# Hartley-transform layer and Sobel layer on one core: a straight and folded first pass, a reordered second pass

## The chip, the cores and the metric

The kernel runs on one core of one Trainium2 chip. The metric is the device time of the core in microseconds (us), the median over runs. TensorE, VectorE, ScalarE, GpSimd and SyncE appear in the profile as PE, DVE, ACT, POOL and SP; PEld is TensorE loading weights.

## The reference

The input x is 32 x 64 planes of 128 x 128 float32 pixels. Two layers are added to it, one behind the other:

```
def reference(x, L0_conv_weights1):
    x = x + _L0_conv_ref(_gn(x), L0_conv_weights1)
    x = x + _L1_conv_ref(_gn(x))
    return x
```

`_gn` is a group norm over pairs of planes. The first layer takes a normalised 2-D Hartley transform of each plane, keeps 20 x 20 modes, mixes them over the channels with the weights and transforms back. The second is a depthwise Sobel filter: the square root of the sum of the squares of the two directional derivatives, and 1e-8.

## The kernel before

Three stages follow each other: `pass1` reads every plane and makes its modes and sums, `mix` mixes the modes, `pass2` reads every plane again, adds the first layer, filters and stores. Each stage is a block with one program per engine; semaphores order them. Rows of a plane lie on the 128 partitions.

**pass1** goes over 16 tiles of 128 planes, each in 8 chunks of 16 planes, each chunk in 2 halves (g). Per chunk TensorE does `first_axis` for both halves (L334, into t_ps), a share of the tile before's `second_axis` (L312, into r_ps) and `mirror` for both halves (L343, L345, into z_ps). ScalarE writes the high parts m_hi (L383), the squares (L415) and the copy of t_ps into tmodes (L419). GpSimd writes the low parts m_lo (L279). VectorE sums the squares (L458), multiplies the plane with z_ps into `prod` (L461) and, once per chunk, sums `prod` (L465); once per tile it has the edges (L440 to L449). SyncE loads a chunk ahead into one of 4 slots of xbuf when the chunk's sum is done (L267). All engines run `over_tiles`: tile 0 written out, a hardware loop of 7 rounds of two tiles, tile 15 written out.

**pass2** goes over 256 steps of 8 planes, 32 steps to a pair of tiles. All engines run `over_steps`: step 0, then a loop of 3 rounds of 64 steps, then 63 steps written out. In step r

- TensorE does `second_axis(r+3)` (L962, into v_ps), `first_axis(r+2)` (L974, into y_ps), `across` of step r for halves 0 and 1 (L982), in some steps four `transposes` of coefficients (L950, into the same bank as v_ps), and `down` of step r for both halves (L982). `across(r)` waits for the remainder p_lo of step r, `down(r, h)` for `finish(r-1, h)`.
- ScalarE does `high(r+1)` (L1035, pairs into p_hi), `copy_v(r+3)` (L1041), the squares of across (L1048) and down (L1054) for both halves, and the `roots` (L1061), two operations for each half.
- VectorE does `finish(r-1)` for both halves (L1135, two operations each), `centre(r+2)` (L1104, adds y_ps to the planes), in steps 1 to 11 of a pair `copy_coef` (L1097), in steps 16 to 23 one of eight `coefficients` operations (L1119 to L1125), and `add` for both halves (L1110).
- GpSimd does `low(r+1)` (L924, the remainder: pairs minus p_hi into p_lo) and then `neighbours(r+2)` (L919, the sum of neighbouring columns, into the one buffer `pairs`), which waits for `centre(r+2)` and for its own remainder.
- SyncE stores step r when both halves are finished and loads step r+8 into the same slot.

The orders that matter are these:

```
            def step(i, r):                      # GpSimd, L927
                if not beyond(i, r + 1):
                    low(i, r + 1)
                if not beyond(i, r + 2):
                    pool.wait_ge(lo_ready, at(i, r) + 2)
                    neighbours(i, r + 2)
```

Of the kernel before, what the change touches and what calls it, by code (L numbers as in the profile page):

```python
# [54 lines left out]
COEF_STEP = 16  # L55
# [134 lines left out]
def pass1(nc, sb, ps, sem, mat, x_p, mats, first, xbuf, modes, rows, late, small, mats_d, first_d, second_d):  # L190

    ctx = ExitStack()
    with ctx:
# [6 lines left out]
        prod = sb(ctx, "prod", [128, 2, CHUNK, 64])  # L200

# [25 lines left out]
        mirrored = sem("p1_mirrored")  # L227
        edge_muled = sem("p1_edge_muled")
# [28 lines left out]
        def _(sp):  # L257
# [6 lines left out]
            with sp.Fori(0, NCHUNK // SLOTS - 1) as j:  # L264
                for s in range(SLOTS):

                    sp.wait_ge(chunk_done, j * SLOTS + s + 1)  # L267
                    load_chunk(sp, xbuf[:, s], x_p, j * SLOTS + s + SLOTS, x_in[s])

        @block.gpsimd  # L270
        def _(pool):
            for part in (x_hi, x_lo):
                nc.gpsimd.memset(part[:, :, :, 0:RIGHT:RIGHT - 1].bitcast(FP32), 0.0).then_inc(padded, 1)

            def tile(i, par):
                for k in range(CHUNKS):
                    for g in range(2):
# [3 lines left out]
                                                x_hi[:, g, :, 1:65].bitcast(FP32), ALU.subtract).then_inc(lo_ready, 1)  # L281

            over_tiles(pool, tile)

        @block.tensor
        def _(pe):
# [74 lines left out]
            over_tiles(pe, tile)  # L361
# [66 lines left out]
        def _(dve):  # L428
# [21 lines left out]

            def tile(i, par):
                for k in range(CHUNKS):
                    slot = k % SLOTS
                    xs = xbuf[:, slot]
                    for g in range(2):
# [4 lines left out]
                        dve.wait_ge(pe_mirror, i * HALVES + 2 * k + g + 3)  # L460
                        nc.vector.tensor_tensor(prod[:, k % 2, HALF * g:HALF * (g + 1), 0:64],  # L461
                                                xs[:, HALF * g:HALF * (g + 1), 0:64][:, :, ::-1],
                                                z_ps[g][:], ALU.mult).then_inc(mirrored, 1)
# [6 lines left out]
            over_tiles(dve, tile)  # L470
            edges(TILES - 1, 1)
# [320 lines left out]
def pass2(nc, sb, ps, sem, mat, x_p, out_p, mats, xpad, modes, rows, corner, mscale, x_in):  # L792

    ctx = ExitStack()
    with ctx:
# [9 lines left out]
        pairs = sb(ctx, "pairs", [128, HALF, W + 2])  # L805
# [22 lines left out]
        pe_t0 = sem("p2_pe_t0")  # L828
# [45 lines left out]
        def group(i, r):  # L874

            g = r % PSTEPS - 1
# [34 lines left out]
        def _(pool):  # L911
# [4 lines left out]
            def neighbours(i, r):  # L916
                pool.wait_ge(centred, at(i, r) + 1)
                plane = xpad[:, r % XSTEPS]
                nc.gpsimd.tensor_tensor(pairs[:, :, 0:W + 1], plane[:, :, 0:W + 1], plane[:, :, 1:W + 2],  # L919
                                        ALU.add).then_inc(paired, 1)  # L920

            def low(i, r):
                pool.wait_ge(hi_ready, at(i, r) + 1)
                nc.gpsimd.tensor_tensor(p_lo[:, r % 2, :, 0:W + 1], pairs[:, :, 0:W + 1],  # L924
                                        p_hi[:, r % 2, :, 0:W + 1].bitcast(FP32), ALU.subtract).then_inc(lo_ready, 1)
# [9 lines left out]
            neighbours(0, 0)  # L935
            low(0, 0)
            pool.wait_ge(lo_ready, 1)
            neighbours(0, 1)
# [3 lines left out]
        def _(pe):  # L942
            def transposes(i, r, g):

                t = pair_of(i, r) + 1
                if g == 0:
                    pe.wait_ge(coef_ready, t + 1)
# [49 lines left out]
            pe.wait_ge(coef_ready, 1)  # L997
            for g in range(TGRP):
# [5 lines left out]
                mm.then_inc(pe_t0, 1)  # L1004
# [8 lines left out]
            def step(i, r):  # L1013
                s = r % PSTEPS
# [12 lines left out]
            over_steps(pe, step)  # L1027

        @block.scalar
        def _(act):  # L1030
            def high(i, r):
# [3 lines left out]
                nc.scalar.activation(p_hi[:, r % 2, :, 0:W + 1], pairs[:, :, 0:W + 1], ACT.Copy).then_inc(hi_ready, 1)  # L1035
# [28 lines left out]

            for g in range(1, TGRP, 2):
                act.wait_ge(pe_t0, g + 1)
# [8 lines left out]
            def step(i, r):  # L1075
                if not beyond(i, r + 1):
                    high(i, r + 1)
                if not beyond(i, r + 3):
                    copy_v(i, r + 3)
# [3 lines left out]
                square_down(i, r, 1)  # L1083
                roots(i, r, 0)
# [5 lines left out]
        def _(dve):  # L1090
            V = nc.vector

            def copy_coef(i, r, g):
                t = pair_of(i, r) + 1
                n = min(4, NB - 4 * g)
                dve.wait_ge(pe_t, (t - 1) * TGRP + g + 1)
# [15 lines left out]
            def coefficients(t, part, q):  # L1112

                n = MODES
                m = modes[:, bass.ds(2 * t + q, 1), :].rearrange("p t (a b) -> p (t a) b", b=n)
# [78 lines left out]
```

## Time and profile before

| | |
|---|---|
| median of 3 runs | 2515.53 us (2514.56 to 2516.2) |
| profiled execution, its own time | 2515.18 us |
| its span | 2513.4 us |
| TensorE busy | 2273.2 us, 90% |
| VectorE busy | 1955.9 us, 78% |
| ScalarE busy | 1953.2 us, 78% |
| GpSimd busy | 1456.1 us, 58% |
| mean granted clock of TensorE | 0.965 |

The span is that from the first to the last instruction. Shares are of the span. A row of the timeline gives the start and the duration in us, the engine, the line, the operation, what it writes and reads, how many like it follow each other (x4: four), and in brackets how long the engine had been idle before it and what ended that. "issue" is a wait for nothing that the profile shows, as for the engine's own instructions. Operations of one engine overlap a little, so that starts, not durations, give the pace.

### The profile page before, as it was taken

The numbers are of one execution on the slowest core, as the hardware profiler recorded it, in microseconds if no ns is written. First come the engines' busy times: TensorE is split into PE (matmuls) and PEld (weight loads), VectorE is DVE, ScalarE is ACT, GpSimd is POOL, SyncE is SP. The second block draws the span as 40 slices with busy tenths as digits, with TensorE's granted clock in tenths as the row PEclk, the third lists the DMA queues.
The fourth block names the chain that finished last, engine by engine and source line by source line (L and its number), as shares of the span: only waits on it lengthen the run. The fifth ranks groups of instructions, "written<-read, shape, count | busy, mean of one in ns | idle before, by whom it ended". The sixth has DMA issues, their size and how long they took to land.

```text
span 2513.4 us, 61005 instructions
## 1 busy us (share of the span) xinstructions
PE 2273.2 (90%) x21212; PEld 1618.4 (64%) x21212; DVE 1955.9 (78%) x2781; ACT 1953.2 (78%) x3633; POOL 1456.1 (58%) x788
## 2 busy tenths in 40 slices
PE   5988988988992687999999999999999999999998
PEld 4777777777782674666665666666666666666665
DVE  5988988988996157887886887887787888877776
ACT  6877877877873325888888888888788888889998
POOL 3433434433433024677676677677677677777776
PEclk9999999999995888999999999999999999999999
DMA  7767666666656321566556566566566556566664
GB/s 204 201 168 202 180 171 190 186 170 185 187 152 131 80 69 51 165 179 180 167 175 176 160 183 180 162 179 185 156 179 178 169 176 182 170 182 180 193 189 138
DMA packets 808903, 421.67 MB, mean 168 GB/s; under 512 B 20912, under 2 KB 807344, under 8 KB 807472
## 3 DMA queue, kind: packets, MB, share of 16 engines
q1 hardware_dynamic: 808624, 417.86, 58.4%
q8 instruction: 186, 3.05, 0.5%
q14 instruction: 93, 0.76, 0.1%
HBM read 283.56 MB, written 134.22 MB: 166 GB/s over the span
## 4 chain that ended last, share of the span: by engine, by line
POOL 21%; ACT 16%; PE 13%; issue 8%; DVE 3%; ACTq 1%; POOLq 0%; DVEq 0%
POOL p_lo L924 12%; POOL pairs L919 9%; PE g_ps L982 9%; ACT p_hi L1035 6%; ACT g_ps L1054 3%; ACT v_sb L1041 3%; DVE g_ps L1110 2%; ACT g_ps L1061 2%; PE v_ps L950 2%; ACT gx L1048 2%; PE y_ps L974 1%; PE v_ps L962 1%; ACTq L1061 0%; ACTq L1045 0%; ACTq L1034 0%
## 5 line engine op out<-in xcount | busy, mean ns | idle before, releaser
L982 PE MATMUL g_ps<-p_hi,stencil 128*128 128x512 f32 x2048 | 867.4, 424 | 16.6 <-DVE xbuf L1135 13.2
L924 POOL TENSOR_TENSOR p_lo<-pairs,p_hi 128x1032 fp32r<-128x1032 f32 x256 | 620.6, 2424 | 387.4 <-ACT p_hi L1035 387.4
L982 PE MATMUL g_ps<-p_lo,stencil 128*128 128x512 f32 x2048 | 818.9, 400 | 0.0
L982 PEld LDWEIGHTS g_ps<-p_hi,stencil 128*128 128x128 f32 x2048 | 387.4, 189 | 339.8 <-issue 158.1
L279 POOL TENSOR_TENSOR m_lo<-xbuf,m_hi 128x512 fp32r<-128x512 f32 x256 | 305.5, 1194 | 438.7 <-ACT m_hi L383 438.7
L919 POOL TENSOR_TENSOR pairs<-xbuf 128x1032 f32<-128x1032 f32 x256 | 488.1, 1906 | 52.9 <-POOL p_lo L924 30.9
L1110 DVE TENSOR_TENSOR g_ps<-gx,g_ps 128x512 f32<-128x512 f32 x512 | 339.4, 692 | 218.5 <-ACT g_ps L1054 217.3
L1135 DVE SCALAR_TENSOR_TENSOR xbuf<-xbuf,rows,g_ps 128x256 f32<-128x256 f32 x1024 | 431.7, 477 | 93.0 <-ACT g_ps L1061 78.6
L1061 ACT ACTIVATE g_ps<-g_ps,rows 128x256 f32<-128x256 f32 x1024 | 401.6, 446 | 112.2 <-DVE g_ps L1110 101.6
L982 PEld LDWEIGHTS g_ps<-p_lo,stencil 128*128 128x128 f32 x2048 | 388.8, 190 | 77.0
L334 PE MATMUL t_ps<-first_sb,xbuf 128*64 128x64 f32 x8192 | 297.9, 229 | 87.8 <-issue 40.4
L334 PEld LDWEIGHTS t_ps<-first_sb,xbuf 128*64 128x64 f32 x8192 | 266.8, 142 | 148.8 <-issue 111.5
L1054 ACT ACTIVATE g_ps<-g_ps 128x512 f32<-128x512 f32 x512 | 288.2, 596 | 85.2 <-PE g_ps L982 85.2
L458 DVE TENSOR_REDUCE rows<-square 128x1024 f32 (+1 forms) x256 | 310.2, 1212 | 43.5 <-ACT square L415 43.5
L1104 DVE TENSOR_TENSOR xbuf<-xbuf,y_ps 128x1024 f32<-128x1024 f32 x256 | 310.8, 1214 | 5.9 <-PE y_ps L974 5.9
L1035 ACT ACTIVATE p_hi<-pairs 128x1032 fp32r<-128x1032 f32 x256 | 274.0, 1070 | 40.5 <-POOL pairs L919 36.1
L1048 ACT ACTIVATE gx<-g_ps 128x512 f32<-128x512 f32 x512 | 278.5, 605 | 2.4 <-PE g_ps L982 2.4
L415 ACT ACTIVATE square<-xbuf 128x1024 f32<-128x1024 f32 x256 | 268.0, 1047 | 5.7 <-DVE rows L458 5.7
L974 PE MATMUL y_ps<-v_sb,mats_sb 41*128 41x512 f32 x1024 | 265.8, 596 | 2.8 <-DVE xbuf L1104 2.8
L383 ACT ACTIVATE m_hi<-xbuf 128x512 fp32r<-128x512 f32 x256 | 161.6, 632 | 105.7 <-PE z_ps L345 105.7
L419 ACT ACTIVATE tmodes<-t_ps 128x328 f32<-128x328 f32 x256 | 188.9, 738 | 30.0 <-PE t_ps L334 30.0
L461 DVE TENSOR_TENSOR prod<-xbuf,z_ps 128x512 f32<-128x512 f32 x256 | 173.4, 677 | 43.7 <-PE z_ps L345 43.7
(114 smaller groups left out, 2341.8 us busy)
## 6 DMA issues: line engine op xcount, KB each, us to landing
xbuf<-x SPq DMA_DIRECT2D x256, 512.0 KB, 5.2
xbuf<-x SPq DMA_DIRECT2D x512, 256.0 KB, 3.1
out<-xbuf SPq DMA_DIRECT2D x512, 256.0 KB, 2.7
xbuf<-weights SPq DMA_DIRECT2D x8, 800.0 KB, 11.5
wmix<-weights SPq DMA_DIRECT2D x8, 800.0 KB, 13.9
second_sb<-second SPq DMA_DIRECT2D x1, 1230.0 KB, 8.4
mats_sb<-mats SPq DMA_DIRECT2D x1, 704.0 KB, 6.4
first_sb<-first SPq DMA_DIRECT2D x1, 32.0 KB, 5.5
```

The costliest lines, as they stand in the source:

```text
L334: mm = nc.tensor.matmul(t_ps[g][side, p, :], xbuf[:, k % SLOTS, HALF * g + p, side], first[:], start=True, stop=True)
L458: nc.vector.tensor_reduce(rows[:, 1, bass.ds(i, 1), p0:p0 + HALF], square[:, g], axis=AX.X, op=ALU.add).then_inc(summed, 1)
L919: nc.gpsimd.tensor_tensor(pairs[:, :, 0:W + 1], plane[:, :, 0:W + 1], plane[:, :, 1:W + 2], ALU.add).then_inc(paired, 1)
L924: nc.gpsimd.tensor_tensor(p_lo[:, r % 2, :, 0:W + 1], pairs[:, :, 0:W + 1], p_hi[:, r % 2, :, 0:W + 1].bitcast(FP32), ALU.subtract).then_i ...
L982: mm = nc.tensor.matmul(g_ps[h][:, axis], stencil[:, m, :], p[:, r % 2, 4 * h:4 * h + 4, o:o + W], start=n == 0, stop=n == len(todo) - 1)
L1035: nc.scalar.activation(p_hi[:, r % 2, :, 0:W + 1], pairs[:, :, 0:W + 1], ACT.Copy).then_inc(hi_ready, 1)
L1048: nc.scalar.activation(gx2[:, h], g_ps[h][:, 0].rearrange("p n w -> p (n w)"), ACT.Square)\
L1054: nc.scalar.activation(f, f, ACT.Square).then_inc(squared_down, 1)
L1061: a = nc.scalar.activation(f, f, ACT.Sqrt, bias=EPS_SOBEL, scale=inv_var[:, bass.ds(group_planes(i, r, h, k), 1)])
L1104: V.tensor_tensor(xs, xs, y_ps[:], ALU.add).then_inc(centred, 1)
L1110: V.tensor_tensor(f, gx2[:, h], f, ALU.add).then_inc(added, 1)
L1135: v = V.scalar_tensor_tensor(xs, xs, mean[:, bass.ds(group_planes(i, r, h, k), 1)], g_ps[h][:, 1, 2 * k:2 * k + 2], ALU.add, ALU.add)
```

## The change

In the first pass TensorE's program is written out for all tiles; GpSimd folds `prod` to half its width (`fold`), a chunk behind, and VectorE sums the folded tile, also a chunk behind; SyncE's loads wait for the products and no longer for the sums. In the second pass TensorE's program is written out; `coefficients` goes to ScalarE, into steps 0 to 7 of a pair and for the next pair, between the squares and the roots (the first pair's are shared by VectorE and ScalarE before the loop); the transposes and their copies go to steps 10 to 20; ScalarE does `copy_v` ahead of `high`; `pairs` has two buffers, and GpSimd does the sum of step r+2 ahead of the remainder of step r+1; VectorE does `centre` between the two halves of `finish`. The core of the diff:

```diff
-COEF_STEP = 16
+COEF_STEP = 0
+T_STEP = 10
...
+        folded = sb(ctx, "folded", [128, 2, CHUNK, 32])
...
-                    sp.wait_ge(chunk_done, j * SLOTS + s + 1)
+                    sp.wait_ge(mirrored, (j * SLOTS + s + 1) * 2 + 2)
...
+            def fold(i, k):
+                pool.wait_ge(mirrored, i * HALVES + 2 * k + 4)
+                if not (is_first(i) and k < 2):
+                    pool.wait_ge(chunk_done, i * CHUNKS + k - 1)
+                p = prod[:, k % 2]
+                nc.gpsimd.tensor_tensor(folded[:, k % 2], p[:, :, 0:32], p[:, :, 32:64], ALU.add).then_inc(fold_done, 1)
...
+                    if k:
+                        fold(i, k - 1)
+                    elif not is_first(i):
+                        fold(i - 1, CHUNKS - 1)
...
-            over_tiles(pe, tile)
+            for i in range(TILES):
+                tile(i, i % 2)
...
+            def sums(i, k):
+                dve.wait_ge(fold_done, i * CHUNKS + k + 1)
+                nc.vector.tensor_reduce(rows[:, 0, bass.ds(i, 1), CHUNK * k:CHUNK * (k + 1)],
+                                        folded[:, k % 2], axis=AX.X, op=ALU.add).then_inc(chunk_done, 1)
...
-                    dve.wait_ge(mirrored, i * HALVES + 2 * k + 4)
-                    nc.vector.tensor_reduce(rows[:, 0, bass.ds(i, 1), CHUNK * k:CHUNK * (k + 1)],
-                                            prod[:, k % 2], axis=AX.X, op=ALU.add).then_inc(chunk_done, 1)
+                    if k:
+                        sums(i, k - 1)
+                    elif not is_first(i):
+                        sums(i - 1, CHUNKS - 1)
...
-        pairs = sb(ctx, "pairs", [128, HALF, W + 2])
+        pairs = sb(ctx, "pairs", [128, 2, HALF, W + 2])
...
-            g = r % PSTEPS - 1
+            g = r % PSTEPS - T_STEP
...
             def step(i, r):
+                if not beyond(i, r + 2):
+                    pool.wait_ge(lo_ready, at(i, r) + 1)
+                    neighbours(i, r + 2)
                 if not beyond(i, r + 1):
                     low(i, r + 1)
-                if not beyond(i, r + 2):
-                    pool.wait_ge(lo_ready, at(i, r) + 2)
-                    neighbours(i, r + 2)
...
-            over_steps(pe, step)
+            for n in range(ALL):
+                step(n // PERIOD, n % PERIOD)
...
+            def coefficients(t, part, q):
+                n = MODES
+                m = modes[:, bass.ds(2 * t + q, 1), :].rearrange("p t (a b) -> p (t a) b", b=n)
...
+                if part == 0:
+                    nc.scalar.activation(coef[:, c0, q, c0], m, ACT.Copy, scale=plus).then_inc(coef_main, 1)
...
+            def corners(t):
+                act.wait_ge(coef_main, t * 2 + 2)
+                nc.scalar.activation(coef[:, 0, :, 0], corner[:, bass.ds(2 * t, 2)], ACT.Copy).then_inc(coef_ready, 1)
+
+            act.wait_ge(coef_zero, 1)
+            for part in range(4):
+                coefficients(0, part, 1)
...
             def step(i, r):
+                if not beyond(i, r + 3):
+                    copy_v(i, r + 3)
                 if not beyond(i, r + 1):
                     high(i, r + 1)
-                if not beyond(i, r + 3):
-                    copy_v(i, r + 3)
                 square_across(i, r, 0)
                 square_across(i, r, 1)
                 square_down(i, r, 0)
                 square_down(i, r, 1)
+                n = r % PSTEPS - COEF_STEP
+                if 0 <= n < 8 and not beyond(i, r - r % PSTEPS + PSTEPS):
+                    if n == 0:
+                        act.wait_ge(pe_t, (pair_of(i, r) + 1) * TGRP)
+                    coefficients(pair_of(i, r) + 1, n // 2, n % 2)
+                    if n == 1:
+                        corners(pair_of(i, r) + 1)
                 roots(i, r, 0)
                 roots(i, r, 1)
...
             centre(0, 0)
             centre(0, 1)
-            for n in range(8):
-                coefficients(1, n // 2, n % 2)
 
             def step(i, r):
-                s = r % PSTEPS
                 if not before(i, r, 1):
                     finish(i, r - 1, 0)
-                    finish(i, r - 1, 1)
                 if not beyond(i, r + 2):
                     centre(i, r + 2)
+                if not before(i, r, 1):
+                    finish(i, r - 1, 1)
                 if group(i, r) is not None:
                     copy_coef(i, r, group(i, r))
-                n = s - COEF_STEP
-                if 0 <= n < 8 and not beyond(i, r - s + 2 * PSTEPS):
-                    coefficients(pair_of(i, r) + 2, n // 2, n % 2)
                 add(i, r, 0)
                 add(i, r, 1)
```

## Rows read from the trace of the kernel before

**Rows 1.** timeline of VectorE, first pass: its sum L465 where a tile ends

```profile
63.61 1.22 DVE L465 TENSOR_REDUCE rows<-prod 128x16 f32<-128x1024 f32 x1
...
665.39 1.22 DVE L465 TENSOR_REDUCE rows<-prod 128x1024 f32 x1
...
707.66 1.22 DVE L465 TENSOR_REDUCE rows<-prod 128x1024 f32 x1
```

**Rows 2.** first pass, who waited for whom: us in total, times, longest us

```profile
DVE prod L461 <- PE z_ps L345: 43.7, 6, 8.1
PE t_ps L334 <- issue: 40.4, 12, 4.0
...
PE t_ps L334 <- ACT tmodes L419: 22.6, 84, 0.3
PE z_ps L343 <- DVE prod L461: 4.4, 15, 0.3
```

**Rows 3.** timeline of GpSimd, a plain step inside the loop of the second pass

```profile
1145.49 2.44 POOL L924 TENSOR_TENSOR p_lo<-pairs,p_hi 128x1032 fp32r<-128x1032 f32 x1 [1.27 <-ACT p_hi L1035]
1148.09 1.91 POOL L919 TENSOR_TENSOR pairs<-xbuf 128x1032 f32<-128x1032 f32 x1 [0.16 <-POOL p_lo L924]
```

**Rows 4.** timeline of TensorE, a plain step behind that loop

```profile
2401.38 0.71 PE L962 MATMUL v_ps<-mats_sb,coef_t 41*128 41x128 f32 x8
...
2402.88 0.51 PE L982 MATMUL g_ps<-p_hi,stencil 128*128 128x512 f32 x1
...
2404.89 0.50 PE L982 MATMUL g_ps<-p_hi,stencil 128*128 128x512 f32 x1
...
2406.97 0.71 PE L962 MATMUL v_ps<-mats_sb,coef_t 41*128 41x128 f32 x8
```

**Rows 5.** page, costly groups: count, busy us, mean ns, idle before, releaser

```profile
L279 POOL TENSOR_TENSOR m_lo<-xbuf,m_hi 128x512 fp32r<-128x512 f32 x256 | 305.5, 1194 | 438.7 <-ACT m_hi L383 438.7
```

**Rows 6.** operations on tile coef: ns min/median/max, first and last start

```profile
L1119 DVE TENSOR_SCALAR coef<-modes,mscale x16: 423/1801/2429, 954.6 to 2059.8; 128x400 f32 x12, 128x400 f32<-128x400 f32 x4
```

**Rows 7.** timeline, a step with transposes inside the loop

```profile
1006.49 0.66 PE L950 MATMUL v_ps<-mats_sb,coef 128*128 128x128 f32 x4 [0.29 <-ACT v_sb L1041]
...
1006.90 0.48 PE L982 MATMUL g_ps<-p_hi,stencil 128*128 128x512 f32 x1
...
1008.13 0.58 ACT L1054 ACTIVATE g_ps<-g_ps 128x512 f32<-128x512 f32 x1 [0.72 <-PE g_ps L982]
...
1008.81 0.70 DVE L1110 TENSOR_TENSOR g_ps<-gx,g_ps 128x512 f32<-128x512 f32 x1 [0.54 <-ACT g_ps L1054]
...
1009.64 1.74 ACT L1061 ACTIVATE g_ps<-g_ps,rows 128x256 f32<-128x256 f32 x4
...
1010.60 0.87 DVE L1135 SCALAR_TENSOR_TENSOR xbuf<-xbuf,rows,g_ps 128x256 f32<-128x256 f32 x2 [0.16 <-ACT g_ps L1061]
```

**Rows 8.** timeline, start of the second pass, a step behind its loop, last centre

```profile
968.13 1.22 DVE L1104 TENSOR_TENSOR xbuf<-xbuf,y_ps 128x1024 f32<-128x1024 f32 x1 [3.63 <-PE y_ps L974]
...
969.50 1.90 POOL L919 TENSOR_TENSOR pairs<-xbuf 128x1032 f32<-128x1032 f32 x1 [15.26 <-DVE xbuf L1104]
...
981.31 1.21 DVE L1104 TENSOR_TENSOR xbuf<-xbuf,y_ps 128x1024 f32<-128x1024 f32 x1
...
2400.42 2.40 POOL L924 TENSOR_TENSOR p_lo<-pairs,p_hi 128x1032 fp32r<-128x1032 f32 x1 [1.18 <-ACT p_hi L1035]
...
2402.39 1.29 DVE L1110 TENSOR_TENSOR g_ps<-gx,g_ps 128x512 f32<-128x512 f32 x2 [1.23 <-ACT g_ps L1054]
...
2403.12 1.54 ACT L1061 ACTIVATE g_ps<-g_ps,rows 128x256 f32<-128x256 f32 x4 [0.35 <-DVE g_ps L1110]
...
2403.96 1.66 DVE L1135 SCALAR_TENSOR_TENSOR xbuf<-xbuf,rows,g_ps 128x256 f32<-128x256 f32 x4 [0.28 <-ACT g_ps L1061]
...
2405.54 1.22 DVE L1104 TENSOR_TENSOR xbuf<-xbuf,y_ps 128x1024 f32<-128x1024 f32 x1
...
2494.86 1.22 DVE L1104 TENSOR_TENSOR xbuf<-xbuf,y_ps 128x1024 f32<-128x1024 f32 x1
```

More of the change, by code:

```diff
@@ L227, in pass1 @@
         mirrored = sem("p1_mirrored")
+        fold_done = sem("p1_fold_done")
         edge_muled = sem("p1_edge_muled")
@@ L281, in tile @@
                                                 x_hi[:, g, :, 1:65].bitcast(FP32), ALU.subtract).then_inc(lo_ready, 1)
+                    if k:
+                        fold(i, k - 1)
+                    elif not is_first(i):
+                        fold(i - 1, CHUNKS - 1)
             over_tiles(pool, tile)
+            fold(TILES - 1, CHUNKS - 1)
         @block.tensor
@@ L460, in tile @@
                         dve.wait_ge(pe_mirror, i * HALVES + 2 * k + g + 3)
+                        if g == 0 and not (is_first(i) and k < 2):
+                            dve.wait_ge(fold_done, i * CHUNKS + k - 1)
                         nc.vector.tensor_tensor(prod[:, k % 2, HALF * g:HALF * (g + 1), 0:64],
@@ L470, in _ @@
             over_tiles(dve, tile)
+            sums(TILES - 1, CHUNKS - 1)
             edges(TILES - 1, 1)
@@ L1034, in high @@
                     act.wait_ge(pe_down, at(i, r) * 2 - 2)
-                nc.scalar.activation(p_hi[:, r % 2, :, 0:W + 1], pairs[:, :, 0:W + 1], ACT.Copy).then_inc(hi_ready, 1)
+                nc.scalar.activation(p_hi[:, r % 2, :, 0:W + 1], pairs[:, r % 2, :, 0:W + 1], ACT.Copy).then_inc(hi_ready, 1)
             def copy_v(i, r):
@@ L1063, in roots @@
                 a.then_inc(rooted, 1)
+            def coefficients(t, part, q):
+                n = MODES
+                m = modes[:, bass.ds(2 * t + q, 1), :].rearrange("p t (a b) -> p (t a) b", b=n)
+                c0, c1, s1 = slice(0, n), slice(1, n + 1), slice(n + 1, 2 * n + 1)
+                plus, minus = (mscale[:, a, bass.ds(2 * t + q, 1)] for a in range(2))
+                if part == 0:
+                    nc.scalar.activation(coef[:, c0, q, c0], m, ACT.Copy, scale=plus).then_inc(coef_main, 1)
+                elif part == 1:
+                    nc.scalar.activation(coef[:, n + 1:2 * n, q, n + 1:2 * n], m[:, 1:, 1:], ACT.Copy, scale=minus)
+                elif part == 2:
+                    nc.scalar.activation(coef[:, s1, q, c1], m, ACT.Copy, scale=minus)
+                else:
+                    nc.scalar.activation(coef[:, c1, q, s1], m, ACT.Copy, scale=minus).then_inc(coef_ready, 1)
+            def corners(t):
[4 more added lines that the diff above has]
+                coefficients(0, part, 1)
             for g in range(1, TGRP, 2):
-                act.wait_ge(pe_t0, g + 1)
+                act.wait_ge(pe_t, g + 1)
                 n = min(4, NB - 4 * g)
@@ L1141, in _ @@
             for part in range(4):
-                for q in range(2):
-                    coefficients(0, part, q)
+                coefficients(part)
             for n, m in enumerate(("smooth", "smooth_neg", "diff")):
```

37 lines of the change are left out of this document (16 added, 21 removed).

## The prediction

> **What bounds the kernel now.** I read the stages first (busy time by window), then each stage's steps in the timeline. The first pass (22 to 757 us) is 16 tiles of 8 chunks, the second (968 to 2513 us) is 256 steps. By the table above TensorE is busy for 90% of the span, VectorE and ScalarE for 78%, GpSimd for 58%. None is so far ahead that its busy time alone would set the end: in each stage I look for the ring of waits that closes on itself once a step.
>
> *First pass.* VectorE's sum L465 ends each tile. A tile inside the loop's body takes 42.27 us (665.39 to 707.66), and the 14 looped tiles from 63.61 to 707.66 take 644.05 us [rows 1]. 14 x 42.27 is 591.8, so 52.3 us are extra. They lie where TensorE's loop jumps back: it waits for nothing but its own code 12 times, 40.4 us in sum, and VectorE stands before L461 six times, 43.7 us, 7.3 each, until TensorE is back [rows 2]. Six jumps, 8.7 us each. Between them TensorE waits 22.6 us for ScalarE's copy of t_ps (84 times) and only 4.4 us for VectorE's product [rows 2]: VectorE looks full, but hardly ends a wait.
>
> *Second pass, plain step in the loop.* VectorE, ScalarE and TensorE follow GpSimd here: it does remainder L924 (1145.49, 2.44 us), sum L919 (1148.09, 1.91 us), and waits 1.27 us for ScalarE's p_hi before the next remainder [rows 3]. With one buffer of sums this ring is closed: 2.44 + 0.16 + 1.91 + 1.27 = 5.78 us. Behind the loop (steps 192 to 255) TensorE goes 2401.38, 2402.88, 2404.89, 2406.97 without a wait listed on it [rows 4]: 5.59 us is its own packed step. So two buffers can give a plain loop step 0.19 us at most, before TensorE is the bound.
>
> **The change, part by part.** The sum is made against the profiled execution, 2515.18 us (span 2513.4 and 1.8 around it); the median of the runs is 2515.53, 0.35 more.
>
> *First pass straight on TensorE.* The six jumps go. ScalarE, VectorE and GpSimd still loop, but VectorE's gap there is a wait for TensorE's z_ps [rows 2], not for its own code. Gain 52.3, taken as -52. Bounds: -40 (what TensorE's own code waits sum to) and -55.
>
> *Fold.* Per chunk GpSimd gets an addition of 128x512: nearest row the remainder L279, 1.19 us. GpSimd stands idle 438.7 us over 256 of those [rows 5], 3.4 per chunk, so it is hidden; without that cover it would cost 1.2 x 128 = 153 us. VectorE's 1.22 us sum [rows 1] is halved, and its wait for its own product goes: some 0.7 us per chunk off an engine for which TensorE waits 4.4 us in all. What VectorE gives up is taken by the wait for ScalarE's copy, which stays. Gain -2 (bounds 0 and -6). SyncE's loads are released a sum earlier; no wait for a load is among the waits, so 0.
>
> *Coefficients.* Before the loop, 8 VectorE operations become 4 beside 4 on ScalarE: -1. The second eight, which stood behind centre(1), go into steps 0 to 7 of the loop. In the steps, VectorE's 1.8 us (median of L1119, 0.42 at best [rows 6]) leave it. On ScalarE I take 0.45: its square of 512 elements is 0.58 [rows 7], 400 elements are fewer, and operations overlap by 0.1. Bounds 0.35 and 1.8. The row shows the same VectorE operation at 0.42 us while GpSimd rests and 1.8 beside it. The Trainium skill (SBUF, State Buffer, section on the two separate sides) says that VectorE and GpSimd take an exclusive lock on a shared port pair and that ScalarE never waits on anyone; by that rule ScalarE's time is the usual one, and no row before shows ScalarE at this work. If the slowness lies in the strided data instead, it is 1.8 on ScalarE too. The sum goes by 0.45; the other is a rival below, worth +38 us.
>
> *Order of the second pass: here the price lies.* GpSimd's step r was: remainder of r+1, sum of r+2. Now it is sum of r+2, **then** remainder of r+1. TensorE's across(r+1) waits for that remainder. So it now also waits for centre(r+2), which sits on VectorE behind finish(r-1,0), which needs down(r-1,0). Follow one round from down(r-1,0), start to start:
> - to ScalarE's square 1.23 (1006.90 to 1008.13; I take 1.24), to VectorE's add 0.68, to the root 0.83, to finish 0.96 [rows 7]: 3.71;
> - finish of half 0, two of four operations, to centre: (2405.54-2403.96)/2 = 0.79 [rows 8];
> - centre to the sum: 968.13 to 969.50, GpSimd idle and waiting for it, 1.37 [rows 8];
> - sum to remainder: 1.91 [rows 3] and a gap that no row shows; bounds 0 and 0.16 (the gap in the other order); I take 0.02, since the wait is met long before: 1.93;
> - remainder to across: 2400.42 to 2402.88 with 2.40 in the operation [rows 4, 8], so 0.06 behind it; with 2.42 in it 2.48;
> - across to down(r+1,0): 2402.88 to 2404.89, 2.01 [rows 4].
>
> Sum 12.29 us, and it has led from down(r-1) to down(r+1): two steps. **No step can be shorter than 6.14 us**, where the loop's plain step was 5.78 and TensorE's packed one 5.59. Before, the same path ran over three steps (the remainder of r+2 needed the sum of r+2), near 4.8 us, and bound nothing. The second buffer is there, but the order spends it; moving half 1 of finish behind centre saves 0.79 of the round and is in the sum. ScalarE is not on this ring except for squares and roots: copy of v first costs nothing and takes away the transposes' wait for it, for v_ps is their tile too; the ring then takes what this gives.
>
> Steps with a transpose put four transposes (0.41, 1006.49 to 1006.90 [rows 7], and 0.09 of turn-round) between across and down, once per round: +0.25, 6.39. Their VectorE copy (1.1 us) ends before the add is due. Steps with coefficients: root 0 must wait for square 1, which starts some 0.95 behind square 0 (half of 2.01, less a turn-round), then 0.49 and 0.45: 1.89 where it was 0.68 + 0.83 = 1.51 [rows 7], so +0.38 on a round, +0.19 a step; 6.33. Behind the loop add to root is 0.73 and root to finish 0.84 [rows 8], 0.10 and 0.12 less: -0.11 a step.
>
> A pair in the loop: 13 x 6.14 + 11 x 6.39 + 8 x 6.33 = 200.7; six of them 1204. Pair 6, behind the loop, 197; pair 7, 31 intervals x 6.03 = 187. Sum 1588. The start is shorter than that by some 5: today the third centre comes at 981.31, 13.2 us behind the first [rows 8], behind eight coefficients. The two jumps back of this pass stay for the other three engines: 3 us in all (bounds 0 and 2 x 7.3 [rows 2]). So 1586 from the first centre to the last, against 2494.86-968.13 = 1527 [rows 8]: +59, and +2 at the end, where the last remainder comes later.
>
> TensorE written out in this pass: its own jumps are in the 1527, so they are not counted again.
>
> **Sum:** 2515.2 - 52 - 2 - 1 + 61 = 2521 us, 0.2% above the median. 0.2% (5 us) is about what a measurement here can tell from no change.
>
> **The rivals.**
> - *Likeliest: the ring of 12.29 us.* 2521; its own range 2508 to 2534 (0.05 us a step is 13 us). Chance 0.45. For it: every link but one is a row, and a ring is a floor that nothing else in the kernel can lower.
> - *Slower: GpSimd pays its loop waits on the ring.* In the loop its gap behind its own operation is 0.16 [rows 3], and the centre to sum link is from a place before the loop [rows 8]. If each of the two GpSimd starts of a round costs 0.1 more, a step is 0.11 longer over the 192 looped steps: +22, 2543. Each 0.01 of added gap is 1.9 us, so it decides from the first hundredths on. Chance 0.22.
> - *Faster: the links are as short in the loop as behind it*, since VectorE and ScalarE are no longer pressed: -0.11 x 192 = -21, 2500. Chance 0.18.
> - *Faster: the order does not bind*, because centre comes early enough; then TensorE bounds at 5.59: 255 x 5.59 + 77 x 0.5 = 1464, -63, so 2397. Against it: centre stands behind finish in VectorE's program. Chance 0.08.
> - *Slower: the coefficients take 1.8 us on ScalarE too*: (1.8-0.45)/2 x 56 steps = +38, 2559. Chance 0.07.
>
> **The numbers.** Left out of the range are the last two, 0.15: 2490 to 2553. Faster by over 0.2%: 0.18 + 0.08 + 0.06 of the likeliest = 0.32. Within: 0.22. Slower: 0.22 + 0.07 + 0.17 = 0.46.
>
> **What would show it.** In the changed profile: no code waits of TensorE at tile changes, and the first pass some 54 us shorter; GpSimd's fold between two remainders without a wait behind it. In the second pass centre to centre 6.1 to 6.2 in plain steps, TensorE idle 0.5 us before across with the remainder as releaser, GpSimd waiting for VectorE's centre and not for ScalarE. Wrong would be: plain steps at 5.6 (the ring does not exist), a wait for centre that is long over when the sum starts, coefficients over 1 us on ScalarE, or new code waits in the straight first pass.

## The result, and the profile after

The changed kernel takes 2495.31 us (median of 4 runs, 2493.35 to 2496.31) against 2515.05 us for the kernel before, run beside it (4 runs): a ratio of 0.9921, 95% interval 0.9907 to 0.9935. It is 20 us faster; the forecast was 6 us slower. The measured time lies in the range of 2490 to 2553 us, on the other side of no change than the likeliest case.

First the page of the changed kernel: its span, the engines' busy time, and four of the costliest groups (busy us, mean ns | idle before, releaser).

```profile
span 2493.9 us, 61110 instructions
PE 2227.6 (89%) x21212; PEld 1619.0 (65%) x21212; DVE 1803.3 (72%) x2714; ACT 2011.3 (81%) x3700; POOL 1593.9 (64%) x916
...
L1007 PE MATMUL g_ps<-p_hi,stencil 128*128 128x512 f32 x2048 | 852.2, 416 | 115.4 <-POOL p_lo L950 107.7
...
L945 POOL TENSOR_TENSOR pairs<-xbuf 128x1032 f32<-128x1032 f32 x256 | 488.2, 1907 | 492.7 <-DVE xbuf L1159 492.6
...
L950 POOL TENSOR_TENSOR p_lo<-pairs,p_hi 128x1032 fp32r<-128x1032 f32 x256 | 609.4, 2380 | 1.7 <-ACT p_hi L1060 1.7
...
L290 POOL TENSOR_TENSOR m_lo<-xbuf,m_hi 128x512 fp32r<-128x512 f32 x256 | 305.6, 1194 | 225.7 <-ACT m_hi L400 224.5
```

No engine is fuller than TensorE's 89%, and TensorE now stands before across (L1007) 107.7 us for GpSimd's remainder. GpSimd no longer waits for ScalarE's p_hi ahead of the remainder, as in [rows 3]; it waits 492.6 us ahead of the sum, for VectorE's centre L1159. That is the wait that the forecast had put on the ring.

The first pass, who waited for whom between 60 and 700 us (us in total, times, longest us), against [rows 2]:

```profile
POOL m_lo L290 <- ACT m_hi L400: 192.5, 219, 1.7
DVE rows L481 <- ACT square L432: 94.5, 119, 1.0
ACT m_hi L400 <- PE z_ps L361: 89.1, 106, 1.4
...
PE t_ps L350 <- ACT tmodes L436: 28.0, 105, 0.3
DVE prod L486 <- PE z_ps L361: 11.4, 31, 0.6
```

TensorE's 40.4 us of waits for its own code are gone, and VectorE's six gaps of 7 us with them; what stays is the wait for ScalarE's copy. The granted clock changed too. In the kernel before it fell to the lower of its two levels, 1.2 GHz, at each of the six jumps, where TensorE stood twice for 2.4 to 4.0 us, and stayed there for 6.8 or 10.2 us, 48 us in all; in the changed kernel it did not fall between 30 and 700 us. The windows of this pass, before and after (us, busy us of PE, PEld, DVE, ACT, POOL with counts, granted clock, DMA share, GB/s):

```profile
30.00:757.00 727.00, 657.69 (x11818) 542.52 (x11816) 633.99 (x704) 577.12 (x947) 301.99 (x253) 0.96 0.66 181
30.00:705.00 675.00, 644.77 (x11834) 532.84 (x11830) 557.75 (x702) 575.88 (x950) 462.10 (x382) 1.00 0.71 195
```

The fold and the tile ends, in the operations on tile folded and in VectorE's timeline (its second sum of squares of a tile, one tile apart):

```profile
L284 POOL TENSOR_TENSOR folded<-prod x128: 1267/1290/1308, 32.3 to 697.1; 128x512 f32<-128x512 f32 x128
...
616.41 1.22 DVE L481 TENSOR_REDUCE rows<-square 128x1024 f32 x1 [0.34 <-ACT square L432]
...
658.54 1.22 DVE L481 TENSOR_REDUCE rows<-square 128x8 f32<-128x1024 f32 x1 [0.40 <-ACT square L432]
```

This tile takes 42.13 us, 42.27 before [rows 1], and all looped tiles are alike: none is longer where a loop would have jumped.

The second pass, one round of two plain steps in the loop, from the timeline:

```profile
1278.68 1.91 POOL L945 TENSOR_TENSOR pairs<-xbuf 128x1032 f32<-128x1032 f32 x1 [1.63 <-DVE xbuf L1159]
...
1279.10 0.39 PE L1007 MATMUL g_ps<-p_hi,stencil 128*128 128x512 f32 x1
...
1280.22 0.58 ACT L1079 ACTIVATE g_ps<-g_ps 128x512 f32<-128x512 f32 x1 [0.33 <-PE g_ps L1007]
...
1280.55 2.39 POOL L950 TENSOR_TENSOR p_lo<-pairs,p_hi 128x1032 fp32r<-128x1032 f32 x1
...
1280.91 0.70 DVE L1165 TENSOR_TENSOR g_ps<-gx,g_ps 128x512 f32<-128x512 f32 x1 [1.52 <-ACT g_ps L1079]
...
1281.74 1.76 ACT L1086 ACTIVATE g_ps<-g_ps,rows 128x256 f32<-128x256 f32 x4
...
1282.69 0.87 DVE L1188 SCALAR_TENSOR_TENSOR xbuf<-xbuf,rows,g_ps 128x256 f32<-128x256 f32 x2
...
1282.99 0.51 PE L1007 MATMUL g_ps<-p_hi,stencil 128*128 128x512 f32 x1 [0.34 <-POOL p_lo L950]
...
1283.48 1.22 DVE L1159 TENSOR_TENSOR xbuf<-xbuf,y_ps 128x1024 f32<-128x1024 f32 x1
...
1284.78 1.91 POOL L945 TENSOR_TENSOR pairs<-xbuf 128x1032 f32<-128x1032 f32 x1 [1.85 <-DVE xbuf L1159]
...
1286.64 2.38 POOL L950 TENSOR_TENSOR p_lo<-pairs,p_hi 128x1032 fp32r<-128x1032 f32 x1
```

The ring can be read off start by start. From down (1279.10; a row of down's later matmuls looks the same, it is the ninth behind across at 1277.10) to square 1.12, add 0.69, root 0.83, finish 0.95, centre 0.79, sum 1.30, remainder 1.86; then remainder to across 2.44 (1280.55 to 1282.99), across to down 2.00. Together 11.98 us for two steps. The steps alternate (5.86 and 6.11 us in one pair of tiles, 5.65 and 6.33 in another), with a mean of 5.99. Behind the loop the mean is 5.92.

By stages, from the starts of centre in VectorE's timeline. A pair of tiles is 32 steps:

| | before | after | forecast change | change |
|---|---|---|---|---|
| start to first centre | 968.13 | 915.53 | -55 | -52.6 |
| first to last centre | 1526.73 | 1558.25 | +59 | +31.5 |
| last centre to the end | 18.5 | 20.1 | +2 | +1.6 |
| of it: pair in the loop, no jump | 193.2 | 196.1 | +7.5 | +2.9 |
| pair 6, behind the loop | 187.1 | 194.3 | +10 | +7.2 |
| pair 7 (31 intervals) | 173.0 | 183.4 | +14 | +10.3 |

So 52.6 us were gained ahead of the first centre, and 33 given back behind it.

### The profile page after: what moved, and what is told of

Same layout as the page of the kernel before. It is cut to its first block, busy times and chain, and to the rows that moved or that the text cites. A ratio compares the mean times of both kernels' runs of the same rounds, so it can differ in the third digit from the quotient of the medians.

```text
span 2493.9 us, 61110 instructions
## 1 busy us (share of the span) xinstructions
PE 2227.6 (89%) x21212; PEld 1619.0 (65%) x21212; DVE 1803.3 (72%) x2714; ACT 2011.3 (81%) x3700; POOL 1593.9 (64%) x916
## 4 chain that ended last, share of the span: by engine, by line
PE 21%; POOL 21%; DVE 10%; ACT 6%; issue 5%; DVEq 1%; POOLq 0%; ACTq 0%
PE g_ps L1007 20%; POOL p_lo L950 12%; POOL pairs L945 9%; DVE xbuf L1159 6%; ACT g_ps L1079 3%; DVE xbuf L1188 3%; ACT g_ps L1086 2%; DVE g_ps L1165 1%; PE v_ps L975 1%; DVEq L1188 0%; DVE coef L1192 0%; ACT gx L1073 0%; PE y_ps L999 0%; ACT coef_t L1116 0%; PE g_ps L1027 0%
## 5 line engine op out<-in xcount | busy, mean ns | idle before, releaser
L1007 PE MATMUL g_ps<-p_hi,stencil 128*128 128x512 f32 x2048 | 852.2, 416 | 115.4 <-POOL p_lo L950 107.7
L1007 PE MATMUL g_ps<-p_lo,stencil 128*128 128x512 f32 x2048 | 815.0, 398 | 0.0
L945 POOL TENSOR_TENSOR pairs<-xbuf 128x1032 f32<-128x1032 f32 x256 | 488.2, 1907 | 492.7 <-DVE xbuf L1159 492.6
L1007 PEld LDWEIGHTS g_ps<-p_hi,stencil 128*128 128x128 f32 x2048 | 386.4, 189 | 417.8 <-POOL p_lo L950 322.6
L1165 DVE TENSOR_TENSOR g_ps<-gx,g_ps 128x512 f32<-128x512 f32 x512 | 356.5, 696 | 360.3 <-ACT g_ps L1079 360.3
L950 POOL TENSOR_TENSOR p_lo<-pairs,p_hi 128x1032 fp32r<-128x1032 f32 x256 | 609.4, 2380 | 1.7 <-ACT p_hi L1060 1.7
L1188 DVE SCALAR_TENSOR_TENSOR xbuf<-xbuf,rows,g_ps 128x256 f32<-128x256 f32 x1024 | 445.5, 476 | 60.4 <-ACT g_ps L1086 40.8
L290 POOL TENSOR_TENSOR m_lo<-xbuf,m_hi 128x512 fp32r<-128x512 f32 x256 | 305.6, 1194 | 225.7 <-ACT m_hi L400 224.5
L1007 PEld LDWEIGHTS g_ps<-p_lo,stencil 128*128 128x128 f32 x2048 | 386.6, 189 | 77.6
L1079 ACT ACTIVATE g_ps<-g_ps 128x512 f32<-128x512 f32 x512 | 298.3, 583 | 168.8 <-PE g_ps L1007 165.2
L1086 ACT ACTIVATE g_ps<-g_ps,rows 128x256 f32<-128x256 f32 x1024 | 410.0, 445 | 24.9 <-DVE g_ps L1165 0.6
L350 PEld LDWEIGHTS t_ps<-first_sb,xbuf 128*64 128x64 f32 x8192 | 259.8, 138 | 116.1 <-issue 70.4
L1159 DVE TENSOR_TENSOR xbuf<-xbuf,y_ps 128x1024 f32<-128x1024 f32 x256 | 310.9, 1214 | 7.9 <-PE y_ps L999 7.9
L1073 ACT ACTIVATE gx<-g_ps 128x512 f32<-128x512 f32 x512 | 289.1, 610 | 12.5 <-PE g_ps L1007 10.9
L987 PEld LDWEIGHTS v_ps<-mats_sb,coef_t 41*128 41x128 f32 x2048 | 135.1, 187 | 98.5 <-issue 95.6
```

The lines of the kernel that those rows point to most:

```text
L290: nc.gpsimd.tensor_tensor(x_lo[:, g, :, 1:65], xbuf[:, k % SLOTS, HALF * g:HALF * (g + 1), 64:], x_hi[:, g, :, 1:65].bitcast(FP32), ALU.su ...
L350: mm = nc.tensor.matmul(t_ps[g][side, p, :], xbuf[:, k % SLOTS, HALF * g + p, side], first[:], start=True, stop=True)
L945: nc.gpsimd.tensor_tensor(pairs[:, r % 2, :, 0:W + 1], plane[:, :, 0:W + 1], plane[:, :, 1:W + 2], ALU.add).then_inc(paired, 1)
L1007: mm = nc.tensor.matmul(g_ps[h][:, axis], stencil[:, m, :], p[:, r % 2, 4 * h:4 * h + 4, o:o + W], start=n == 0, stop=n == len(todo) - 1)
L1073: nc.scalar.activation(gx2[:, h], g_ps[h][:, 0].rearrange("p n w -> p (n w)"), ACT.Square)\
L1079: nc.scalar.activation(f, f, ACT.Square).then_inc(squared_down, 1)
```

## The experiments

Of each kernel the time is the median, and the ratio is to the kernel before, run on the same chip; that took 2513.9 to 2514.4 us each time.

**GpSimd's order, undone.** The forecast's ring exists only because the sum goes ahead of the remainder.

```diff
-                if not beyond(i, r + 2):
-                    pool.wait_ge(lo_ready, at(i, r) + 1)
-                    neighbours(i, r + 2)
                 if not beyond(i, r + 1):
                     low(i, r + 1)
+                if not beyond(i, r + 2):
+                    pool.wait_ge(lo_ready, at(i, r) + 1)
+                    neighbours(i, r + 2)
```

> GpSimd's order put back (remainder of r+1, then sum of r+2), the two buffers kept; nothing else changed. Theory (the ring of two steps over sum, remainder, across, down, square, add, root, finish, centre sets the step, 11.98 us a round in the changed kernel's profile): that ring falls back to three steps and another closes, remainder, sum, ScalarE's copy, remainder, 2.4 + 1.9 + 1.27 = 5.6 us: plain steps 5.6 to 5.65 us, the whole 2400 to 2420 us. Rival (the steps are long because ScalarE now carries the coefficients and GpSimd loops): plain steps stay at 6.0 us, the whole within 10 us of 2495.

2422.27 us, ratio 0.9636 (0.962 to 0.9652): 73 us less than the change, 2 us over the expected range. Its waits of the second pass (960 to 2400 us):

```profile
POOL p_lo L950 <- ACT p_hi L1060: 382.1, 247, 4.7
DVE g_ps L1165 <- ACT g_ps L1079: 275.0, 495, 3.3
ACT g_ps L1079 <- PE g_ps L1007: 116.6, 319, 1.1
PEld g_ps L1007 <- POOL p_lo L950: 94.8, 125, 0.8
```

GpSimd's wait is for p_hi again, and the wait that stopped TensorE's matmuls before across is gone. Plain steps take 5.62 us on average in the loop (5.54 to 5.69) and 5.47 behind it. The order of two operations on an engine that is busy for 64% of the span is worth 73 us, more than the whole first pass gained.

**Centre behind both halves of finish.** This makes one link of the ring longer by a known size.

```diff
                     finish(i, r - 1, 0)
+                    finish(i, r - 1, 1)
                 if not beyond(i, r + 2):
                     centre(i, r + 2)
-                if not before(i, r, 1):
-                    finish(i, r - 1, 1)
```

> VectorE's centre put back behind both halves of finish; nothing else changed. Theory (ring of two steps): a round gets two more operations of finish, 0.79 us, so a step 0.39 us: plain steps 6.4 us, the whole 2495 + 255 x 0.39 = 2590 to 2600 us. Rival (centre comes early enough, VectorE is idle 28% of the span): within 10 us of 2495.

2694.15 us, ratio 1.073 (1.0702 to 1.0759): +199 where some +100 was expected. At the end of the pass the ring does as it should: steps of 6.63 and 6.15, 12.78 a round, against 5.62 and 6.23, 11.85, in the change: +0.93. Before that, in the loop and in pair 6 behind it, rounds take 12.9 to 15.6 us. The windows of this kernel (us, busy us of PE, PEld, DVE, ACT, POOL with counts, granted clock, DMA share, GB/s):

```profile
1200.00:1400.00 200.00, 173.05 (x828) 117.22 (x829) 131.29 (x210) 151.13 (x287) 119.64 (x58) 0.93 0.51 151
2400.00:2600.00 200.00, 173.63 (x880) 115.63 (x877) 132.55 (x220) 165.58 (x313) 133.18 (x63) 1.00 0.56 165
```

and its operations of L1007 in the first of them:

```profile
L1007 PE MATMUL g_ps<-p_hi,stencil x226: 390/402/796, 1200.6 to 1399.7; 128*128 128x512 f32 x113
```

Around the rounds of 12.78 us the granted clock is 1.00; in the window of longer ones it is 0.93, with matmuls of 796 ns where 402 is usual: at times the lower level, 1.2 GHz. TensorE stood up to 2.6 us for the remainder there. The trace sorts the 127 rounds of the pass. 53 of them ran wholly at the full clock, and are 0.96 us longer than the same rounds of the change, near the 0.93 of the ring. In the other 74 the clock was at the lower level for 201 us in all, and they are 1.90 us longer each. So the ring accounts for some 120 us, and the other 70 lie in the rounds with the lower clock. That TensorE's idle time brought the clock down fits these rows, but no run kept the one and not the other.

**Centre ahead of both halves.**

```diff
+                if not beyond(i, r + 2):
+                    centre(i, r + 2)
                 if not before(i, r, 1):
                     finish(i, r - 1, 0)
-                if not beyond(i, r + 2):
-                    centre(i, r + 2)
-                if not before(i, r, 1):
                     finish(i, r - 1, 1)
```

> VectorE takes the centre ahead of both finishes instead of between them. The centre then starts behind the add of its step and not behind root and first finish, so the ring sum, remainder, across, down, centre loses root and finish (0.95 + 0.79 us, less the time of V and Y that the centre also waits for on TensorE): a round of two steps falls from 11.98 us to what the other ways leave, about 11.4 to 11.6, thus 2440 to 2460. Rival: the centre is held by TensorE's Y (which waits for V's copy) and not by the finish ahead of it, and nothing changes: 2490 to 2500.

2429.87 us, ratio 0.9663 (0.9647 to 0.9679), with GpSimd's new order kept. Plain steps are 5.76 us, all alike, 11.52 a round as expected; the total is 10 us below the expected 2440 to 2460, because steps with transposes fell too, from 6.22 to 5.95. That the steps are alike says that what binds now closes once a step:

```profile
1265.74 1.22 DVE L1159 TENSOR_TENSOR xbuf<-xbuf,y_ps 128x1024 f32<-128x1024 f32 x1
...
1266.88 1.65 DVE L1188 SCALAR_TENSOR_TENSOR xbuf<-xbuf,rows,g_ps 128x256 f32<-128x256 f32 x4
...
1267.79 0.19 PEld L1007 LDWEIGHTS g_ps<-p_hi,stencil 128*128 128x128 f32 x1 [0.46 <-DVE xbuf L1188]
...
1270.42 1.03 PE L999 MATMUL y_ps<-v_sb,mats_sb 41*128 41x512 f32 x4
...
1271.50 1.22 DVE L1159 TENSOR_TENSOR xbuf<-xbuf,y_ps 128x1024 f32<-128x1024 f32 x1
```

Centre to finish 1.14, to down 0.91, through both downs and V to Y 2.63, to centre 1.08: 5.76. With centre ahead of finish, the ring through the remainder no longer binds.

**Centre a step further ahead.** V of r+4, Y and centre of r+3, copy of V of r+4; nothing else. Cut to its core:

```diff
-                if not beyond(i, r + 2):
-                    centre(i, r + 2)
+                if not beyond(i, r + 3):
+                    centre(i, r + 3)
```

> Second and first axis on TensorE, the copy of v and centre all one step further ahead (r+4 and r+3 in step r); GpSimd's order as in the changed kernel. Theory: centre of r+2 is done a step before GpSimd's sum of it asks, the ring runs over three steps (about 4 us a step) and nothing but TensorE's packed 5.6 us is left: plain steps 5.6 us, steps with transposes 6.1 us, the whole about 2400 us (255 x 5.6 + 77 x 0.5 against 1558 us from first to last centre). Rival (GpSimd's two operations in this order are the bound by themselves, or ScalarE is): steps of 5.9 us or more, the whole over 2470 us.

2419.89 us, ratio 0.9629 (0.9613 to 0.9645). The ring is cut at another place, and 75 us come back where the other cut gave 73. Plain steps are 5.6 us as expected; the total is 20 us over the expected 2400, since steps with coefficients still take 6.05.

**Coefficients behind the roots.** In the change they stand between the squares and the roots. Three kernels move them: the change itself, the one with centre further ahead, and the one with GpSimd's old order.

```diff
+                roots(i, r, 0)
+                roots(i, r, 1)
                 n = r % PSTEPS - COEF_STEP
...
-                roots(i, r, 0)
-                roots(i, r, 1)
```

> ScalarE's coefficient operation of a step stands behind the roots and no longer ahead of them; nothing else changed. Theory: it leaves the ring (steps 0 to 7 of a pair are 6.25 us against 5.99 in plain ones): 56 steps x 0.2 to 0.25 us = 11 to 14 us less, about 2483 us. Rival (ScalarE's load itself lengthens these steps, wherever the operation stands): within 3 us of 2495.

> e9 with ScalarE's coefficients issued behind its roots instead of ahead of them. If a coefficient costs because it stands between the square and the roots of its step, which are on what is left of the ring, the 56 steps with one fall from 6.03 us to about 5.7: 17 us less than e9, about 2403. If they are long because ScalarE then has more work in the step than TensorE, whatever the order, the step moves its length elsewhere and the gain is a few us, as in e10: 2414 to 2420.

> e1 (GpSimd takes the remainder ahead of the next sum) with the coefficients behind the roots. The same two answers as for e11: about 2405 if their place on the way to the roots is what costs, 2415 to 2420 if it is ScalarE's load.

2489.83 us (ratio 0.9901, 0.9885 to 0.9918), 2419.39 us (0.9618, 0.9602 to 0.9635) and 2415.54 us (0.9607, 0.9591 to 0.9623): 5.5, 0.5 and 6.7 us less than the same kernels with the coefficients between, about the resolution. The first lies between its theory (11 to 14 us less) and its rival (within 3); the other two came out as expected if ScalarE's load is what costs. The place costs little; the load is the better account. ScalarE in a coefficient step of the last of them:

```profile
1136.59 0.60 ACT L1066 ACTIVATE v_sb<-v_ps 128x512 f32<-128x512 f32 x1
1137.07 1.07 ACT L1060 ACTIVATE p_hi<-pairs 128x1032 fp32r<-128x1032 f32 x1
1138.03 1.09 ACT L1073 ACTIVATE gx<-g_ps 128x512 f32<-128x512 f32 x2
1138.98 1.10 ACT L1079 ACTIVATE g_ps<-g_ps 128x512 f32<-128x512 f32 x2
1140.54 1.54 ACT L1086 ACTIVATE g_ps<-g_ps,rows 128x256 f32<-128x256 f32 x4 [0.46 <-DVE g_ps L1165]
1141.98 0.67 ACT L1101 ACTIVATE coef<-modes,mscale 128x400 f32 x1
1142.51 0.61 ACT L1066 ACTIVATE v_sb<-v_ps 128x512 f32<-128x512 f32 x1
```

From copy of V to copy of V 5.92 us, of which it waits 0.46: with a coefficient its own list is 5.46 us long. The one wait is for VectorE's add, which itself waits for ScalarE's square. List and wait fill the step, so each operation in the list counts, wherever it stands. This kernel is the fastest of all that ran, 3.9% below the kernel before and 80 us below the change.

**The high part ahead of the copy of V again.**

```diff
-                if not beyond(i, r + 3):
-                    copy_v(i, r + 3)
                 if not beyond(i, r + 1):
                     high(i, r + 1)
+                if not beyond(i, r + 3):
+                    copy_v(i, r + 3)
```

> The high part is made ahead of the copy of V again, one part of the change undone. The ring of two steps goes over neither: GpSimd's remainder waits for the high part, but that is made while the next sum runs on GpSimd. The copy of V comes 0.7 us later, and TensorE wants it only with its next step, so 0 to +8 us, 2495 to 2503. Rival: TensorE's wait for V returns in the steps with transposes, +15 us.

2511.36 us, ratio 0.999 (0.998 to 0.9999), +16 where 0 to +8 was expected: the rival was right. Waits of its second pass:

```profile
PEld v_ps L975 <- ACT v_sb L1066: 44.2, 70, 0.7
...
PE v_ps L975 <- ACT v_sb L1066: 13.4, 68, 0.3
```

Steps with transposes are 6.43 us, not 6.22. The transposes lie between across and down, on the ring, so what they wait, a round pays.

**TensorE's loops put back, one pass at a time.**

```diff
-            for i in range(TILES):
-                tile(i, i % 2)
+            over_tiles(pe, tile)
```

> The changed kernel with TensorE's program of the first pass put back into its loop; all else as changed. Theory (straight code removes the six jumps back, 8.7 us each, and the fold nothing): 2495 + 50 to 54, about 2547 us. Rival (the fold is worth a good part of the first pass's gain, since VectorE's sum was over 1 us a chunk): less than +35 us.

```diff
-            for n in range(ALL):
-                step(n // PERIOD, n % PERIOD)
+            over_steps(pe, step)
```

> The changed kernel with TensorE's program of the second pass put back into its loop. Theory (a round of the ring measures 11.98 us instead of the 12.29 summed, because links differ by their neighbours: no turn-round of TensorE ahead of down, GpSimd's next operation issued while the last one ends): only the two jumps cost, +2 to +6 us, 2497 to 2501. Rival (TensorE's waits against constants instead of registers shorten the links): +0.15 us a step over 192 looped steps, about 2525 us.

First pass looped: 2556.27 us, ratio 1.0163 (1.0146 to 1.018), +61 where some +52 was expected. Its waits between 60 and 700 us:

```profile
DVE prod L485 <- PE z_ps L361: 69.5, 32, 10.6
PE t_ps L350 <- issue: 51.0, 12, 4.6
```

The 12 waits for code are back, 51.0 us where they were 40.4 in the kernel before, and so are six falls of the granted clock, 58 us at the lower level where it was 48. Why these waits are longer here, no run shows. Second pass looped: 2511.24 us, ratio 0.9987 (0.9977 to 0.9997), +16, between expectation and rival. The two pairs with a jump take 205.0 and 203.6 us instead of 198.3 and 198.1 (+12), the other pairs in the loop 197.35 instead of 196.1, +1.25 each.

**No fold.** VectorE sums prod at full width, a chunk behind; GpSimd does not fold.

```diff
-                dve.wait_ge(fold_done, i * CHUNKS + k + 1)
+                dve.wait_ge(mirrored, i * HALVES + 2 * k + 4)
...
-                                        folded[:, k % 2], axis=AX.X, op=ALU.add).then_inc(chunk_done, 1)
+                                        prod[:, k % 2], axis=AX.X, op=ALU.add).then_inc(chunk_done, 1)
```

> The changed kernel without the fold: VectorE sums the whole product again, a chunk behind, GpSimd has only its remainders in the first pass. Theory (TensorE's ring with ScalarE, over mirror, high part, square and copy of t_ps, sets 42.2 us a tile): 0 to +3 us, 2495 to 2498. Rival (VectorE, at 4.81 us a chunk and 2.4 for the edges, would bound once TensorE does not jump): +0.3 us a chunk or more, 2530 us or over.

2498.66 us, ratio 0.9938 (0.9921 to 0.9954), +3.4, at the edge of what can be told. In the first pass 15 tiles take 630.1 us instead of 628.6, so 1.5 us of it at most is the fold's; the first centre even starts 1.6 us earlier without it (913.9 against 915.5), and the rest lies behind the first centre, unexplained. 128 operations on GpSimd and 74 us less of VectorE (1877.6 busy without, 1803.3 with) move the time by as good as nothing, since VectorE does not end waits here.

**Only the second buffer, in the kernel before.**

```diff
-        pairs = sb(ctx, "pairs", [128, HALF, W + 2])
+        pairs = sb(ctx, "pairs", [128, 2, HALF, W + 2])
...
-                    pool.wait_ge(lo_ready, at(i, r) + 2)
+                    pool.wait_ge(lo_ready, at(i, r) + 1)
```

> The kernel before with two buffers of sums and nothing else: same order on GpSimd, the sum waits for its remainder of a step before instead of the one just done. Theory: the ring remainder, sum, ScalarE's copy, remainder stays closed by GpSimd's own order, only the gap of 0.16 us goes: plain steps 5.75 to 5.6 us, steps with transposes and coefficients as before, the whole 12 to 18 us under the kernel before, about 2500. Rival (the single buffer was the bound): a gain of 35 us and more.

2506.52 us, ratio 0.9966 (0.9956 to 0.9977), -8 where 12 to 18 less was expected. Plain steps go from 5.75 to 5.54 in the loop and from 5.58 to 5.47 behind it, but once a pair a step takes 7.76 us instead of 6.1, 10 us over the six pairs, about what is missing. The timeline of that step, here and then in the kernel before:

```profile
1126.34 2.03 POOL L919 TENSOR_TENSOR pairs<-xbuf 128x1032 f32<-128x1032 f32 x1
...
1126.53 1.87 DVE L1128 COPY coef<-corner 128x2 f32 x1
```

```profile
1124.74 0.15 DVE L1128 COPY coef<-corner 128x2 f32 x1
1124.76 1.91 POOL L919 TENSOR_TENSOR pairs<-xbuf 128x1032 f32<-128x1032 f32 x1 [0.16 <-POOL p_lo L924]
```

A copy of two elements a partition, 156 ns by its median in the kernel before, lasts 1.87 us and ends with GpSimd's sum, which started 0.19 us ahead of it. In the kernel before GpSimd's gap of 0.16 us let the copy start some 0.01 us ahead of the sum, and it was short; the second buffer takes that gap away. By the Trainium skill (SBUF, State Buffer, section on the two separate sides) a VectorE operation in a two-port mode and one of GpSimd hold their shared port pair as an exclusive lock for the whole instruction, and the one that starts second is blocked; the rows agree, 1.87 us instead of 0.16.

## Why the forecast missed

- *First pass straight, -52.* Right: -52.6 to the first centre, where -55 stood for all three terms (-52, -2, -1); undone alone, +61. Undoing costs 8 us more than the change gained, and the waits for code are 11 us longer in that kernel (51.0 against 40.4). The forecast saw only the waits at a jump (6.7 us of its 8.7); the granted clock also fell at each.
- *Fold -2, hidden on GpSimd.* Hidden, as said; a gain of -2 is not shown, since without the fold the tiles are 1.5 us longer in all and the first centre no later. A fold lasts 1.29 us where 1.2 was taken, and GpSimd's idle time before m_lo fell from 438.7 us [rows 5] to 225.7 beside it.
- *Coefficients 0.45 on ScalarE.* Near: an operation lasts 0.59 to 0.64 us and takes 0.49 to 0.54 from start to start, not 1.8 as on VectorE [rows 6]. The kernel before shows why VectorE was slow: 51 of its 64 scalings started while GpSimd's remainder ran, and every one ended 0.21 to 0.23 us behind it; the other 13 took 0.40 to 0.43. The effect on a step was +0.26 (6.25 against 5.99), not +0.19.
- *The ring of two steps.* The mechanism was right, link by link, and both kernels that cut it within the second pass (old order 73 us, centre ahead 75 us) take it away. **What failed is the size of the sum, 12.29 us a round; it is 11.98.** The terms:

| link | forecast | measured |
|---|---|---|
| down to square | 1.24 | 1.12 |
| to add, root, finish | 0.68, 0.83, 0.96 | 0.69, 0.83, 0.95 |
| finish to centre | 0.79 | 0.79 |
| centre to sum | 1.37 | 1.30 |
| sum to remainder | 1.93 | 1.86 |
| remainder to across | 2.48 | 2.44 |
| across to down | 2.01 | 2.00 |

  Most of the 0.31 us lies in three terms. Down to square came from [rows 7], a step whose down started right behind transposes with a matmul of 0.48 us; in a plain step it is 0.39, and TensorE never turned round. Centre to sum came from the first sum of the pass [rows 8], when GpSimd had been idle for 15 us. And for the sum to remainder the bounds were "0 and 0.16" of gap: below nothing was left out, though the forecast itself says that operations of one engine overlap; they overlap by 0.05. Behind the loop root and finish came 0.08 and 0.12 sooner, as forecast, but centre to sum takes 1.36 there, so a step fell by 0.06 and not by 0.11.
- *What that was worth.* 0.155 us a step and near 250 steps: 39 us by the ring alone. A pair in the loop came to 196.1 instead of 200.7, so six of them 28 us less than forecast; pairs 6 and 7 another 6; the 5 us between this and 39 are the coefficient steps (0.09 us over 56 steps). Against it, the start of the pass was not 5 us shorter, and the jumps back cost 4.2 us, not 3. That is the 27.5 us by which the second pass missed; with 0.4 at its end, and less the 2.4 us that the first pass fell short of -55, it is the miss of the whole, 2521 against 2495.7 in the profiled execution. The sign turned on it, since a gain of 53 and a loss of 61 had been set against each other.
- *The rivals.* "Links as short in the loop as behind it" (2500) was nearest by its number, and by luck: the two links that it counted on, to root and to finish, stayed 0.83 and 0.95 in the loop where they are 0.75 and 0.84 behind it, and others were shorter. "GpSimd pays its loop waits on the ring" fell: centre to sum is 1.29 in the loop and 1.36 behind it, sum to remainder 1.86 in both. Its sum was off as well, since twice 0.1 a round is 0.10 a step and +19 us, not 0.11 and +22. "The order does not bind" fell by the run with the old order.
- *"TensorE written out in this pass ... not counted again".* This was wrong in its reason. Undone alone it is +16: a looped TensorE pays its jumps on the ring, 12 us, and its other steps are 0.04 us longer; that this comes from waits against registers is not shown. The forecast put the jumps of the other three engines at 3, which held (4.2), so the sum did not suffer.
- *Copy of V first costs nothing and the ring takes what it gives.* The first half holds; the second does not: with the old order of the two the transposes' wait is on the ring, and the time is 16 us longer.
- *"5.59 us is its own packed step", so the second buffer gives 0.19 at most.* Wrong: with the second buffer alone the steps behind the loop, too, fall from 5.58 to 5.47, so what [rows 4] showed was not TensorE's packed step, and in the loop the buffer gave 0.21.

The parts undone one at a time: centre behind both halves +199, first pass looped +61, second pass looped +16, high first +16, no fold +3, GpSimd's old order -73. That is +222 in all, where the kernel before is 20 us slower: they do not add up, since several share one ring. The place of centre is worth so much only because GpSimd's new order put centre on a ring of two steps.

## What to carry to other kernels

A second buffer and an order that spends it are two changes: ask of the new order which operation now waits for a later one's input, and follow the ring through all engines to where it closes, over how many steps. If a loss from such a ring and a gain elsewhere are of one size, the sign hangs on hundredths of a microsecond per link: take every link from a step of the kind that is counted, start to start, and give each a bound on both sides. When a ring binds, move the operation that feeds it ahead in its own engine's program before trading more work between engines.

## What the runs showed of the hardware that was not expected

- A tiny operation of VectorE can last as long as GpSimd's beside it: 156 ns to 1.87 us.
- TensorE's jumps back in the first pass cost different waits in different kernels: 40.4 us for six in the kernel before, 51.0 in the change with the loop put back. At each the granted clock fell to the lower level as well, for 6.8 or 10.2 us.
- VectorE's scalings of 361 or 400 elements ended 0.21 to 0.23 us behind the GpSimd operation that they started in, 1.55 us or more instead of 0.40 to 0.43; ScalarE took 0.65 at most for them.
- A step behind the loop can be shorter than the 5.59 us of [rows 4]: 5.47 with GpSimd's old order, and with the second buffer alone.
- A ring that is 0.93 us longer a round cost 199 us where 127 rounds give 118; the excess lies in the 74 rounds in which the granted clock was at the lower level for a while.
- Here the ring over two steps shows as steps that alternate (5.65 and 6.33) about its half; the one over one step shows as steps that are alike (5.76).
